# Where the spread of B stands in the tensor engine's order, in a state-space scan with a mixture-of-experts behind it

## What is computed

```
dt = softplus(dt_param @ W_dt.T + b_dt) + 1e-05
A_disc = exp(-exp(A_log) * dt[..., None])          # 256 features x 16 states
Bx = Bp[:, :, None, :] * dt[..., None] * xs[..., None]
s = A_t * s + Bx_t                                 # along the tokens
y = C * s.sum(-1) + D_param * xs
out = (y @ W_out.T) * silu(z)
```

## Time and profile before

| what | us |
| --- | --- |
| median of 3 runs | 1149.19 |
| lowest and highest run | 1149.02, 1155.79 |
| the execution that was profiled | 1153.47 |
| its span in the profile | 1151.7 |

### The profile page before, as it was taken

One profiled execution on the slowest core, in us unless ns is written; L12 is line 12 of the kernel. 1 busy time (PEld: TensorE's weight loads), 2 busy tenths in 40 slices (PEclk: granted clock), 3 DMA queues, 4 the chain that ended last, 5 costly groups with the idle time before them and its releaser, 6 DMA issues.

```text
span 1151.7 us, 15570 instructions
## 1 busy us (share of the span) xinstructions
PE 1016.1 (88%) x4732; PEld 823.8 (72%) x4732; DVE 656.9 (57%) x1150; ACT 640.5 (56%) x1240; POOL 673.1 (58%) x658
## 2 busy tenths in 40 slices
PE   7676399696985977988989999999999999999996
PEld 4324176564753756767767888899999999999885
DVE  7898989999998897987896442111111111111045
ACT  5786869688685786697573442233333333333244
POOL 0764958859489998599787237643333333332233
PEclk9798689798896987999899999999999999999998
DMA  6710010202002008132643477599999888886262
GB/s 200 247 37 1 23 51 19 73 1 90 3 1 92 1 1 267 46 87 62 160 142 67 147 237 211 105 268 293 322 324 309 288 270 270 271 265 193 45 205 98
DMA packets 142276, 166.84 MB, mean 145 GB/s; under 512 B 26456, under 2 KB 127088, under 8 KB 142048
## 3 DMA queue, kind: packets, MB, share of 16 engines
q1 hardware_dynamic: 126512, 147.12, 39.4%
q0 software_dynamic: 15680, 18.72, 8.7%
HBM read 139.46 MB, written 26.77 MB: 144 GB/s over the span
## 4 chain that ended last, share of the span: by engine, by line
PE 54%; POOL 15%; ACT 10%; issue 9%; DVE 9%; DVEq 0%; POOLq 0%; ACTq 0%
PE psum L1245 23%; PE psum L1212 13%; POOL Ssum L1931 8%; PE psum L1224 7%; PE psum L1201 5%; DVE S L1472 4%; ACT A L1773 3%; POOL list_d L1950 3%; PE psum L1167 2%; DVE psum L1433 1%; PE psum L1188 1%; ACT hT L1834 1%; ACT hT L1817 1%; PE psum L1127 1%; POOL xs L1896 1%
## 5 line engine op out<-in xcount | busy, mean ns | idle before, releaser
L1931 POOL TENSOR_TENSOR Ssum<-Ssum,S 128x512 f32<-128x512 f32 x217 | 272.4, 1277 | 70.4 <-DVE S L1472 69.6
L1245 PE MATMUL psum<-w,hT 128*128 128x256 f32 x1136 | 252.3, 379 | 0.5 <-issue 0.5
L1981 POOL DMA_INDIRECT acc_d<-y,ID x71 | 113.1, 1593 | 219.4 <-DMA acc_d<-y,ID 115.1
L1245 PEld LDWEIGHTS psum<-w,hT 128*128 128x128 f32 x1136 | 213.3, 190 | 29.1 <-issue 0.9
L1212 PE MATMUL psum<-XT,w 128*128 128x256 f32 x800 | 181.8, 384 | 3.6 <-issue 2.4
L1212 PEld LDWEIGHTS psum<-XT,w 128*128 128x128 f32 x800 | 153.2, 192 | 28.0 <-issue 4.6
L1773 ACT ACTIVATE A<-dts,nea 128x512 f32<-128x512 f32 x245 | 164.9, 719 | 11.6 <-DVE S L1472 8.4
L1433 DVE TENSOR_TENSOR psum<-us,psum 128x512 f32<-128x512 f32 x234 | 149.1, 683 | 17.5 <-PE psum L1118 17.2
L1828 ACT ACTIVATE y<-psum,ID 128x256 f32<-128x256 f32 x71 | 29.9, 472 | 214.5 <-DVE psum L1607 214.5
L1472 DVE TENSOR_TENSOR_SCAN S<-A,carry,psum 128x512 f32<-128x512 f32 x120 | 148.5, 1266 | 0.0
L1607 DVE TENSOR_TENSOR psum<-bb,psum 128x256 f32<-128x256 f32 x71 | 27.0, 425 | 195.8 <-PE psum L1245 195.8
(11 more groups left out here) (185 smaller groups left out, 1340.7 us busy)
## 6 DMA issues: line engine op xcount, KB each, us to landing
w<-W SPq DMA_DIRECT2D x92, 1024.0 KB, 7.0
bb<-b SPq DMA_DIRECT2D x46, 128.0 KB, 7.1
xnb<-x SPq DMA_DIRECT2D x16, 256.0 KB, 3.0
Xr<-x SPq DMA_DIRECT2D x16, 256.0 KB, 5.2
x_d<-gb SPq DMA_DIRECT2D x8, 512.0 KB, 3.4
xn_d<-nb SPq DMA_DIRECT2D x8, 512.0 KB, 4.2
X<-x_d SPq DMA_DIRECT2D x16, 256.0 KB, 8.6
ACC<-acc_d SPq DMA_DIRECT2D x16, 256.0 KB, 5.6
```

The source lines that it names most:

```text
L1245: t = eng.matmul(bank(g)[:, 256 * k:256 * k + 256], hT[n % 2][:, f, 128 * k:128 * k + 128], w[:, f, :], start=f == 0, stop=f == 7)
L1931: eng.tensor_tensor(to, to, of, ALU.add).then_inc(nsum, 1)
L1981: eng.indirect_dma_start(acc_d, bass.IndirectOffsetOnAxis(ap=ID[:, col, 1:2].bitcast(u32), axis=0), y[n % NY][:, k, :], None, compute_op=A ...
```

## The change

At even k, the row `spread` of the next state is written behind the scan's row and behind what the ending, the preparation and the routing have due at this k; before, it stood in front of the multiplication and the scan of this k. It still stands in front of the experts' rows. Only PE acts on this row. The second edit reads the pause between the routing's tables from `TABLE_REST[min(r, 1)]`; the table has two equal entries, and the third round is only reached when the pause isn't read.

```diff
@@ -262,8 +262,6 @@
             decay_until(m + AHEAD + 1 if k > LAST_PREP else min(m + AHEAD + 1, 32 * i + 32))
-            if k % 2 == 0 and m + 2 < 32 * NC:
-                say("spread", *divmod(m // 2 + 1, 16))
             if k % 2 == 0:
                 say("mult", i, k // 2)
             say("scan", i, k)
@@ -352,7 +350,7 @@
             if not past[0]:
-                for _ in range(TABLE_REST[r][n % 2]):
+                for _ in range(TABLE_REST[min(r, 1)][n % 2]):
                     yield
@@ -564,6 +562,8 @@
             part(routing, 1)
+            if k % 2 == 0 and 32 * i + k + 2 < 32 * NC:
+                say("spread", *divmod(16 * i + k // 2 + 1, 16))
             if i:
                 calls = BUSY[i] if listed[0] else CALLS[i]
```

## The result

| | before, us | after, us |
| --- | --- | --- |
| median (16 runs each) | 1151.32 | 1158.57 |
| lowest, highest | 1149.00, 1155.79 | 1152.20, 1159.67 |
| the execution that was profiled | 1153.47 | 1159.30 |
| its span | 1151.7 | 1157.5 |

The ratio is 1.0052, 95% interval [1.0041, 1.0063]: 6.0 us slower by the ratio, where the two medians lie 7.3 us apart. The forecast was 1152.7 (range 1145 to 1160) and 3.5 us slower. Of after's 16 runs, 12 lie between 1157.8 and 1159.7 and 4 between 1152.2 and 1154.1; what sets the two groups apart isn't shown. The profiled execution is of the upper group.

The account below looks back on a forecast made before the run. No engine was taken as full before the last scan, and PE bounds the block behind it. Chunk 0's 2.3 us plus chunks 1 to 3, net of k = 24's gains, gave +3.5 on 1149.2: 1152.7 us, range 1145 to 1160.

Parts of the forecast that it names:

- The frame: Delay of the last scan reaches the end one to one; 30 of 128 spreads move; under 1% counts as no change.
- Chunk 0, +2.3: Spreads behind xT, xc and z in chunk 0 come late: one carried delay of 2.3 us, not three.
- k = 4, +0.6 each: Spread behind wout and xc delays DVE by 0.6 us each in chunks 1, 2, 3 and 5.
- rival C: PE at the low clock at k = 4 of chunks 1, 2, 3, 5: +17, about 1167 us; chance 10%.
- k = 16, +0.7 and +1.4: Spread behind dbc costs 0.7 us in chunk 3 and 1.4 in chunk 5, the latter costed at nothing.
- k = 24, gains of 0.5 and 0.8: nT's second half runs before the spread, so logit comes 0.5 us earlier in chunk 1, 0.8 in chunk 2.
- rival B: Existing waits absorb DVE's delays in chunks 1 to 3, nT's early half gains: -1.5 us, 1148; chance 14%.
- What is hidden: POOL's backlog in chunks 4 to 6 hides late scans, so chunk 5's +0.6 and +1.4 cost nothing.
- Rival A: Nothing is hidden and the 1.3 us gained at k = 24 doesn't arrive: +8.6, 1158 us; chance 14%.
- Rival E: Nothing that can be seen, as 98 of 128 spreads stay: 1149 us; chance 8%.
- Rival D: PE's clock rises before logit and the experts' first matmuls: -10.5 us or 1139, -19 with all five chunks; chance 9%.
- The marks: Right: DVE's spread waits grow by 5 to 8, constant 3 us from 322 us; wrong: DVE's softplus or POOL waits vanish.

Follow-up runs that it names:

- same chip: The kernels before and after the change, profiled once more beside each other on a second chip; last scans at 624.03 and 629.03 us.
- e1: The kernel before, with the spread moved in chunk 0 alone (k = 2, 6, 8, 20); ratio 1.0012 [0.9992, 1.0032].
- before_again: The unchanged kernel before, one execution on another chip than the first pair; 1162.02 us, last scan at 624.03.
- after_again: The changed kernel as it is, run again on another chip than the first pair; ratio to before 1.0048 [1.0022, 1.0073], last scan at 629.03.
- e2: The kernel before, with the spread moved at k = 4 of chunks 1 to 7 alone; ratio 1.0025 [1.0002, 1.0048].
- e6: The changed kernel plus one unused matmul in front of wout, waiting for the scan the spread had waited for; ratio to before 1.0024 [0.9993, 1.0054].
- e3: The kernel before, with the spread moved at k = 16 and 18 (behind dbc, dt) alone, from chunk 1 on; ratio 0.9998 [0.9974, 1.0022].
- e4: The kernel before, with the spread moved at k = 24 (behind nT's second half) of chunks 1 to 7 alone; ratio 0.9994 [0.9970, 1.0019].
- e9: The kernel before, order untouched, plus unused matmuls in front of nT, xT and wout; ratio 0.9921 [0.9897, 0.9946], 1156.27 us.
- e10: The changed kernel plus unused matmuls in front of nT, xT and wout; ratio to before 0.9982 [0.9962, 1.0002], 1163.59 us.

## Why the prediction was nearly right, step by step

**The frame held.** In the first pair the end follows the last scan one to one, no other spreads moved, and the time is in the range and within 1%. The size was too small: 3.5 us against 5.8 (first profile), 5.0 (same chip) and 6.0 (ratio). That 1158.57 lies 5.9 us over the forecast of 1152.7 is in part the base: 1149.19 was a median of 3, and that of 16 is 1151.32.

**Chunk 0, +2.3.** 1.2 us in the first pair, 2.6 (same chip) and 2.2 (e1) later. One delay, as said, carried through chunk 1's start. The first pair came out lower since PE's clock happened to rise sooner in after, within the second half of xT: these four matmuls took 0.62 us there (row below), 1.06 in before and in e1. So xc and its spread came a microsecond sooner than my 51.1. The other two lean the other way: before_again's four took 0.85 us. Held against the first before, after_again and e1 are 2.0 and 1.6 us late.

```profile
44.51 0.62 PE L1056 MATMUL psum<-C,xnb 128*128 128x128 f32 x4
```

**k = 4, +0.6 each: the step that failed, in chunk 1.** Chunks 2, 3 and 5 gave 0.76, 0.63 and 0.63 in the first pair. Chunk 1 gave 3.3 (first pair), 2.3 (same chip) and 2.3 (e2). I wrote that what precedes wout "isn't changed except for one spread of 0.4 us". That one spread parted the wait. Its end reads 2.77 us idle, a matmul, 0.29 us idle; without it 3.45 us in one piece. With e6's filler in its place the cost is 0.57. So the term is mis-sized by 1.7 to 2.7 us, and that is the clock's part: rival C's mechanism at one place, where it had been priced for four at 3.7 each. In the first profile of after it also occurs in chunk 7 (wout 3.75 us behind an idle time of 3.69 us), where scans go from 4.7 to 5.6 us late; the forecast had nothing there.

**k = 16, +0.7 and +1.4.** Chunk 3 gave 1.9 in the first pair (2.2 with what arose just before) and nothing in after_again and e3: the slack there depends on the clock at which the experts' matmuls in front ran (16 in 6.42 us or in 3.62). Chunk 5 gave 1.6, 0.9 and 1.1, and by k = 28 the stream had taken up all of it. Costing it at nothing was right, but the reason given was not what the rows show. It was to wait in POOL's queue; what took it up were DVE's waits for ACT, 1.27 us for softplus and 0.73 for logit in before, which after doesn't have. They come to 2.0 us, and 2.2 were taken up. No row shows POOL's queue taking up a delay, so that this term came out at nothing was luck in part.

**k = 24, gains of 0.5 and 0.8.** The mechanism was right, the sizes are 0.4 and 0.35 (e4). Chunk 1's gain of 2.2 us at k = 28 in the first pair is the old wait of 2.14 us taking up a late stream; this is half of rival B, and it is why a loss of 4.8 us at k = 6 ended as 2.5. In the same-chip pair this wait was 0.51 us in before_again and took up 0.6.

**What is hidden.** From chunk 4, k = 2 (4.5 us in the first pair) to the end the stream moved by 1.4 us more, 0.9 of it at chunk 7's wout. Rival A's 8.6 us was not reached; that its 1158 us is the time measured is chance: the delays of chunk 5 were hidden, and k = 24 did gain, if only 0.75 of its 1.3 us. Rival E is out by the interval. Rival D needs fillers.

**The marks.** Waits of DVE for spreads were to grow by 5 to 8: they grew by 4.7, by 6.6 with L1426 (4.2 and 7.5 in the same-chip pair). "A constant 3 us from 322 us" was 4.5 to 5.8, and 6.7 for a while in chunk 5. One sign of being wrong came true, a wait of DVE for softplus that vanishes; it was the cover of chunk 5.

**Two draws.** The part above 3.5 us may be chance in part. e1 changes nothing at k = 4, its wait there is 2.77 us as in before, yet its wout took 3.24 us. Nor do single profiles add up: the last scans of e1 and e2 are 4.1 and 4.5 us behind before_again's, together more than after_again's 5.0.

**Open.** Why the clock fell behind 2.8 us of idle time in e1, e9 and e10 and not in eight others isn't shown, nor how often it does in either order: each run has one profile, and of the executions behind the ratios no trace was kept. So how much of the 6.0 us is wout's clock, on average, is an inference from single traces. A run with chunk 1's k = 4 alone undone, and one with two separate fillers in wout's wait, weren't made.

## What to carry to other kernels

A cheap instruction that waits in the middle of an idle stretch of PE is not free to move: price the instruction behind it at both clocks, and find the rows with the longest idle time in front of them first. Before moving a step behind others, list which of them it used to hold back or wake, not only which it used to delay. Where PE waits for other engines anyway, matmuls that lead nowhere, put right in front of the work that counts, were worth 0.5 to 0.8% here; no order of the spreads that was tried gained anything clear of noise.

A delay that is hidden is hidden by a certain wait. Name its row and its length, and compare the length with the delay: chunk 5's delays met waits of 2.0 us, and not the ones that the forecast had named.

## What the runs showed of the hardware

**The idle time in front and the clock.** wout of chunk 1 in the 14 profiles, these twelve and the first pair: behind 3.45 us of idle time it ran at the low clock in 3 of 3 (after, after_again, e2: 3.05 to 3.75 us). Behind 2.77 or 2.86 us and a short matmul (in e9 two: spread and filler) it ran at the full clock in 8 (1.96 to 2.00 us) and at the low one in 3 (e1, e9, e10: 3.15 to 3.35 us). The Trainium skill, "TensorE: Matmul & The Clock Gate", Part 1, on oscillation, has matmuls behind each long wait for a transfer begin throttled; the rows agree for a wait of a scan, and with one short matmul within the wait it mostly, not always, stayed away. With 3 cases against 11 this is a tendency, not a rule. The same page of the Trainium skill puts the ramp's penalty below 1% of a typical kernel's span: the fillers of e9 got back 0.8%, which agrees in size; logit in chunk 4 still ran at the low clock there (3.55 us), so it isn't all that there was.

**The same code, another tail.** From 650 to 1100 us the stretch of after_again reads:
```profile
650.00:1100.00 450.00, 437.54 (x2404) 391.76 (x2403) 58.51 (x160) 142.63 (x388) 172.12 (x142) 0.98 0.79 238
```
2404 matmuls in place of 2484, at 0.98 in place of 1.00, while the scans end no later than in the first pair. The same code behind the last scan took 536 to 541 us on these two chips and 523 in the first pair. The loss lies in one place. From 700 to 760 us PE is busy for all 60 us in before and in after, at 1.00. In after_again:
```profile
700.00:760.00 60.00, 49.04 (x205) 39.88 (x204) 4.60 (x10) 12.37 (x30) 34.10 (x32) 0.86 0.57 151
```
PE is idle for 11 us of it and at the low clock for a part; before_again has 52.91 us of busy time at 0.94. Why PE isn't fed there isn't shown. It cancels in a ratio only on average, and not in a difference between chips.

**The same kernel twice.** The scans of before and before_again, two executions of one program, stand 3.1 us apart at the end of chunk 1 and 4.4 at the last scan, nearly all of it gathered in chunks 0 to 2 at the steps where the clock is now low, now full. A change of 3 to 5 us is as large as this draw: it takes the ratio of many runs to see it, and the trace only says where it may arise.
